# Gate stages with bias rows per item and one-hot row choice, and another end of the first mixture

## The reference

```python
x = x + L0_gnn(layernorm(x), edges)      # three message rounds, then attention over nodes
x = x + L0_ffn(layernorm(x))             # 8 experts, hidden 1536, two per node
x = x + L1_gnn(layernorm(x), edges)      # two graph attention layers, 8 heads and 1
x = x + L1_ffn(layernorm(x))             # 4 experts, hidden 384, one per node

# L0_ffn
gates = softmax(x @ Wg + bg)
topg, topi = top_k(gates, 2); topg = topg / sum(topg)
h = gelu(x @ W1[e] + b1[e]);  y = h @ W2[e] + b2[e]
out = sum over the two chosen experts of topg * y
# L1_ffn: the same with argmax of the logits and a share of 1
```

## Time and profile before

| | us |
|---|---|
| median of 3 runs | 1471.71 |
| lowest and highest run | 1467.08, 1474.52 |
| the profiled execution | 1465.52 |
| its span, first to last instruction | 1463.0 |

### The profile page before, as it was taken

How to read it: one execution, slowest core, us unless ns; L and a number is a source line. 1 busy time by engine, 2 the same in 40 slices (tenths; PEclk the granted TensorE clock), 3 DMA queues, 4 the chain that set the end, 5 groups by cost and what they waited for, 6 DMA issues and landing times.

```text
span 1463.0 us, 18209 instructions
## 1 busy us (share of the span) xinstructions
PE 1287.5 (88%) x6567; PEld 1088.3 (74%) x6567; DVE 920.1 (63%) x1748; ACT 560.8 (38%) x981; POOL 127.4 (9%) x114
## 2 busy tenths in 40 slices
PE   5999999999999899986788999999966687967786
PEld 3677489799699766566588999999955587946543
DVE  4477655554644655546459999999965798244213
ACT  2111313413512333450058888888831364010010
POOL 0000200000000000110200000000060563010101
PEclk9999999999999999997599999999987889976699
DMA  9320462203105200313258999999961000010276
GB/s 334 133 86 29 173 216 108 98 1 141 65 1 216 87 1 1 113 40 130 86 216 295 370 379 377 385 371 373 355 225 51 25 1 1 0 65 1 97 253 209
DMA packets 81778, 223.46 MB, mean 153 GB/s; under 512 B 4972, under 2 KB 18348, under 8 KB 81592
## 3 DMA queue, kind: packets, MB, share of 16 engines
q1 hardware_dynamic: 75256, 192.79, 36.1%
q0 software_dynamic: 6464, 29.89, 5.6%
HBM read 195.92 MB, written 26.74 MB: 152 GB/s over the span
## 4 chain that ended last, share of the span: by engine, by line
PE 71%; DVE 16%; DMA 5%; issue 3%; ACT 2%; POOL 2%; ACTq 0%; SPq 0%; DVEq 0%; POOLq 0%
PE dve_ps L720 10%; PE dve_ps L721 10%; PE dve_ps L722 10%; PE dve_ps L763 4%; PE act_ps L720 3%; PE act_ps L721 3%; PE act_ps L722 3%; PE dve_ps L809 3%; DMA slot<-in_e1w 2%; PE act_ps L936 2%; PE dve_ps L953 2%; PE act_ps L760 2%; DVE part_slot L2041 2%; PE dve_ps L1175 2%; DVE part_slot L2032 2%
## 5 line engine op out<-in xcount | busy, mean ns | idle before, releaser
L2032 DVE TENSOR_TENSOR part_slot<-slot,item_hi 128x768 fp32r<-128x768 f32 x156 | 137.7, 951 | 0.9 <-ACT item_hi L1499 0.8
L1499 ACT ACTIVATE item_hi<-slot 128x768 fp32r<-128x768 f32 x156 | 118.0, 838 | 34.2 <-DMA slot<-in_e0w 31.5
L2041 DVE TENSOR_TENSOR part_slot<-slot,item_hi 128x768 fp32r<-128x768 f32 x132 | 116.5, 952 | 0.0
L720 PE MATMUL act_ps<-item_hi,hid_hi 128*128 128x384 f32 x288 | 98.8, 343 | 4.8 <-DVE hid_lo L2209 4.8
L1507 ACT ACTIVATE item_hi<-slot 128x768 fp32r<-128x768 f32 x132 | 100.0, 877 | 7.0 <-DMA slot<-in_e0w 6.8
L720 PE MATMUL dve_ps<-item_hi,x_hi 128*128 128x384 f32 x288 | 98.3, 341 | 2.9 <-DVE part_slot L2032 1.7
L721 PE MATMUL act_ps<-part_slot,hid_hi 128*128 128x384 f32 x288 | 99.0, 344 | 0.0
L722 PE MATMUL act_ps<-item_hi,hid_lo 128*128 128x384 f32 x288 | 97.7, 339 | 0.0
L721 PE MATMUL dve_ps<-part_slot,x_hi 128*128 128x384 f32 x288 | 97.2, 337 | 0.0
L722 PE MATMUL dve_ps<-item_hi,x_lo 128*128 128x384 f32 x288 | 96.9, 337 | 0.0
L1390 ACT ACTIVATE h_t<-act_ps,par 128x256 f32<-128x256 f32 x36 | 21.1, 587 | 122.4 <-PE act_ps L827 122.4
(11 more groups left out here) (395 smaller groups left out, 3254.6 us busy)
## 6 DMA issues: line engine op xcount, KB each, us to landing
slot<-in_e0w SPq DMA_DIRECT2D x48, 2304.0 KB, 10.3
slot<-in_w SPq DMA_DIRECT2D x9, 2304.0 KB, 9.6
slot<-in_e1w SPq DMA_DIRECT2D x12, 1152.0 KB, 6.2
ea_raw<-in_edge SPq DMA_DIRECT2D x8, 1024.0 KB, 5.4
slot<-in_wqkv SPq DMA_DIRECT2D x3, 2304.0 KB, 15.2
item_x<-xs SPq DMA_DIRECT2D x17, 384.0 KB, 9.7
xs<-zrow POOLq DMA_DIRECT2D x2, 3072.0 KB, 15.7
ys<-item_y POOLq DMA_DIRECT2D x16, 384.0 KB, 6.3
```

The source lines that it names most:

```text
L720: mm(to, kept[0], moved[0], start=start, stop=False)
L1499: go(item_hi[j][k][:, :], slot[s][:, k * D:(k + 1) * D], ACT.Copy).then_inc(up_high[j], 1)
L2032: vv.tensor_tensor(part_slot[s][:, ks], slot[s][:, ks], item_hi[j][k][:, :].bitcast(F32), ALU.subtract).then_inc(up_low[j], 1)
L2041: vv.tensor_tensor(part_slot[s][:, ks], slot[s][:, ks], item_hi[j][k][:, :].bitcast(F32), ALU.subtract).then_inc(down_low[j], 1)
```

## The change

**Bias rows.** The stages bias0 and bias1 go: no gates are turned, no biases multiplied or added to x. Instead POOL loads the second bias of an item's expert, one row of 768, to all 128 partitions (`b2row`) after it has issued the store of the item before, and VectorE adds it as it copies the result (waiting for `b2_in`).

**Gate stages by tile.** Tiles are turned one by one (`turn_tile`), copied by ScalarE in two halves, and each tile's logits made apart (`tile_logits`). Stage 0 norms tiles 0 and 1 together, then 2, then 3; stage 1 each alone, with the last weighted sums between the turns. The low parts of the first item's up weights move: slot 2's on VectorE ahead of the additions, slot 3's to POOL. Counts are made in 5 products (`rank_tokens`).

**Row choice.** ScalarE and VectorE keep high and low parts of the normed rows, not turned. `first_sel[0]` is made straight from the counts (the rank within expert 0, and chosen by expert 0) before the rest of the plan; `first_sel[1]` holds item 1's rows. `pick_rows` chooses rows of item 0 and of item 1 with 16 single-pass products of 384 columns each; ScalarE copies them to `item_x`, and TensorE turns them. Item 1 is no longer loaded from DRAM, and the scatters are waited for only before item 2 (in the second mixture before the loop). TensorE's order is: choose 0, turn 0, first up half, choose 1, second up half, turn 1.

**Loop.** Hidden blocks go in the order 0, 1, 2 and not 2, 0, 1; gelu and high part alternate; the second up half waits for all three bent blocks of the item before; the result is taken after three of the six last low parts.

**End of the first mixture, and the products h1 and h2.** VectorE and not POOL makes the low parts of the next weight, six before the first gathered addition and six after it; then the last result, a gathered addition, and the distributed rows tile by tile with statistics; one `rescale` of all four tiles follows. The first unit of h1 and of h2 waits block by block.

```diff
-            def gates(run, xt, ne, stage, bias_stage, b2, k_in):
...
+            def turn_tile(run, t, source, before):
+                pe.wait_ge(normed, before + t + 1)
+                if t >= 2:
+                    pe.wait_ge(kept_act, 7 * run.layer + 2 * (t - 1))
+                for half in range(2):
+                    bank = act_ps[(2 * t + half) % RING]
+                    for j in range(3):
...
+                    turned.then_inc(tile_turned, 1)
...
+            def rank_tokens(run):
+                pe.wait_ge(run.sel_set, 1)
+                ne = run.ne
+                mm(run.count_bank[:, 0:(NT + 1) * ne], tri[:, :], sel[:, :, 0:ne], start=True, stop=False)
+                for t in range(1, NT + 1):
+                    last = mm(run.count_bank[:, t * ne:(NT + 1) * ne], ones[:, :], sel[:, 0:NT + 1 - t, 0:ne], start=False, stop=(t == NT))
+                last.then_inc(counts_ready, 1)
+            def pick_rows(run, i, highs, lows):
...
+                pe.wait_ge(first_set[i], run.layer + 1)
+                for half in range(2):
+                    hs = slice(half * HALF, (half + 1) * HALF)
+                    for m in range(NT):
+                        for part in (highs, lows):
+                            picked = mm(run.pick_banks[half][:, 0:HALF], first_sel[i][:, m, :], part[m][:, hs],
+                                        start=(m == 0 and part is highs), stop=(m == NT - 1 and part is lows))
+                    picked.then_inc(picked_rows, 1)
+            for t in range(3):
+                turn_tile(run0, t, xn1, NT * (L + 1))
...
+            tile_logits(run0, 0, xn1_t)
+            turn_tile(run0, 3, xn1, NT * (L + 1))
+            for t in range(1, NT):
+                tile_logits(run0, t, xn1_t)
...
-                            pe.wait_ge(hid_bent, 3 * (i - 1) + 1)
+                            pe.wait_ge(hid_bent, 3 * i)
...
-                pick_x()
-                times_up(0)
+                pick_rows(run, 0, xn1_hi, xn1_lo)
+                turn_x(0)
+                times_up(0, (0,))
+                pick_rows(run, 1, xn1_hi, xn1_lo)
+                times_up(0, (1,))
                 turn_x(1)
```

```diff
-            normalise(xres, xn1, attention_arrives)
+            low_up(0, 0)
+            for ts in ((0, 1), (2,), (3,)):
+                for t in ts:
+                    for half in range(2):
+                        add_to_x("wo", t, half)
+                    gate_rows(t, xres)
+                rescale(ts, xres, xn1)
+            keep_turned(run0, xn1_t)
+            for t in range(NT):
+                low_rows(run0, t, xn1, xn1_hi, xn1_lo)
...
+                for t in range(NT):
+                    last = vv.tensor_scalar(first_sel[0][:, t, :], slot_iota[:, :], count[:, t, 0:1], sel[:, t, 0:1], ALU.is_equal, ALU.mult)
...
                 def result(i):
                     wait(dve, run.y_out, 16 * i)
+                    dve.wait_ge(run.b2_in, 16 * (i + 1))
                     dve.wait_ge(down_used[1], DC * (i + 1))
                     for half in range(2):
-                        vv.tensor_copy(item_y[:, half * HALF:(half + 1) * HALF], down_banks[half][:, 0:HALF]).then_inc(y_set, 1)
+                        hs = slice(half * HALF, (half + 1) * HALF)
+                        vv.tensor_tensor(item_y[:, hs], down_banks[half][:, 0:HALF], b2row[:, hs], ALU.add).then_inc(y_set, 1)
...
-                    low_up(1, k + 2)
+                    low_up(1, k + 2, range(3))
                     result(k)
+                    low_up(1, k + 2, range(3, DC))
...
+            for i in range(DC):
+                low_first(i)
+            add_gathered(0)
+            for i in range(DC, 2 * DC):
+                low_first(i)
+            last_result()
+            add_gathered(1)
+            result_rows(0)
+            result_rows(1)
+            for t in range(2, NT):
                 add_gathered(t)
-            vv.memset(root[:, 0, :], 0.0).then_inc(parts_added, 1)
-            last_result()
-            normalise(xres, xn2, results_arrive)
+                result_rows(t)
+            rescale(range(NT), xres, xn2)
...
+            def load_b2(run, e):
+                pool.dma_start(b2row[:, :], run.b2[bass.ds(e, 1), :].rearrange("a d -> (a d)").partition_broadcast(P)).then_inc(run.b2_in, 16)
...
+            for k in range(DC):
+                ks = slice(k * D, (k + 1) * D)
+                pool.wait_ge(up_high[1], k + 1)
+                nc.gpsimd.tensor_tensor(part_slot[3][:, ks], slot[3][:, ks], item_hi[1][k][:, :].bitcast(F32), ALU.subtract
+                                        ).then_inc(up_low[1], 1)
...
                 with pool.Fori(1, last) as k:
                     store(k, *stored_at(k))
+                    load_b2(run, expert(k + 1))
```

466 lines of the change are left out of this document (255 added, 211 removed).

## The result

The changed kernel takes 1399.12 us (median of four runs, 1396.34 to 1404.01) where the kernel before took 1469.39 on the same chip: a ratio of 0.9525, 95% interval 0.9501 to 0.9549, faster by 70 us. The forecast (1414, range 1394 to 1441, faster) held, but the time lies 15 us under its centre and 2 over rival (a): the sum of terms was 10.6 us short.

The account below looks back on a forecast made before the run. Gate stages were bound by chained waits between engines, the loop by full TensorE and DMA engines. Terms 30.2 + 8.4 + 4 + 23.7 - 8.5 - 3 = 54.8 us gave 1410.7 or 1416.5 by base; forecast 1414, range 1394 to 1441.

Parts of the forecast that it names:

- rival (a): Bias rows are free and the clock stays up in the gate stages: 11.5 + 6 us more gain, about 1397; 14%.
- Gate stage 0: Before the first loop: logits 7.7 us earlier, counts 4.1, counts to loop 18.4; 30.2 us gained in all.
- The loop: First mixture's items: bias row's 0.39 MB an item at 375 GB/s costs +8.5 us; +3.4 if 385 were the ceiling.
- The end of the first mixture: Last result to h1: first product of h1 8.4 us earlier, 0.7 of it from the first low hidden block coming sooner.
- h2: Product h2 starts 0.8 us after its first low block instead of behind eight: 4 us gained.
- Gate stage 1: Before the second loop: logits about 4.7 us earlier, counts 4.0, counts to first up product 15.0; 23.7 us gained.
- Second loop: Second mixture: five bias rows at 1.0 us each join the loop, half to all showing; +3 us cost.
- (b): In the loop, waiting for three bent blocks couples ScalarE's lateness in: +24 us, about 1438; 17%.
- (c): The loop's bias row lands late, so VectorE's result and TensorE's next down half wait; slower than before, 1480 at 30 us; 5%.
- (d): The loop ends when its loads do, so the early start is given back wholly: 30.2 us back, 1444; 3%.

Follow-up runs that it names:

- low_dve: The changed kernel with slot 3's six low parts made on VectorE instead of POOL; ratio 0.9504 to the kernel before.
- plain4: The changed kernel with three further 0.39 MB loads an item of the first mixture, each reading 128 different rows of expert weights; ratio 0.9735, items 29.47 us apart.
- before_row: The kernel before with one unused bias row loaded for each item of the first mixture on POOL's queue; ratio 1.004, items 27.72 us apart.
- order201: The changed kernel with hidden blocks in the old order 2, 0, 1 and the second up half waiting for one bent block; ratio 0.9517.
- warm: The changed kernel with 14, 14 and 6 unused 384-column products in three idle stretches of TensorE in gate stage 0; ratio 0.948.
- best: The changed kernel with unused TensorE products in both gate stages, slot 3's low parts on VectorE and the first mixture's end norm in two parts; 1391.99 us, ratio 0.9485.

## Why the prediction held, and where it was short

**Gate stage 0** (30.2 predicted, 29.6 measured) is right step by step, to 0.6 us in each: two stretched operations (run low_dve took them away and got 2.25 us back for the 2 that were charged), logits at the lower clock, five products for fourteen, then the dependence of the first item on nothing but the counts. The hidden turn was put 28.8 us behind the counts and came 28.6 behind. That the choice of item 1 pays was in the sum as 2.9 us of TensorE against the load from DRAM; alone it is worth 2.65. The load's 8.78 us of the earlier trace rows were not what there was to win: it runs beside the second up half, and TensorE stood idle for it 3.13 us in the kernel before.

**The loop** is the step that failed. The prediction's "At 375 GB/s, the middle of the loop's slices ..., 10.61 MB take 28.3 us" took a rate that TensorE's pace had asked for (10.22 MB in 27.20 us) as what the queues can give. Plain loads got 401 GB/s over 180 us. The page "DMA: Bandwidth & Descriptors" of the Trainium skill (section Measured), which has about 425 GB/s, was set aside in the prediction for the trace's rate. No run here held that figure in the loop (401 GB/s over 180 us is the most, in plain4), but its answer, that the row is free, was nearer than the one taken. Measured, the row costs 0.5 us an item in the kernel before (5 us in ten items, 5.9 in the ratio) and nothing that can be seen in the changed one. The changed loop loses 1.2 us between item 0's hidden turn and item 11 for 8.5 predicted, and the run without rows shows the same pace. Measured by low hidden parts, items are 27.25 to 27.5 apart in all changed kernels with at most one row. That is neither the row nor the order of blocks, and it is about 1 us in all: at the turns of rows the changed kernel has 27.26 and low_dve, which loads the rows too, (1021.22 - 776.84) / 9 = 27.15, as the kernel before. What makes this 1 us is open. Other differences of the loop (gelu and high part in turn, the result taken between two halves of low parts) were not tried alone, and of the kernel before there is one trace. Why this loop hides a row that the one before does not is open for the same reason. Two sums of the prediction were also off: at 385 GB/s its own terms give 10.61 / 0.385 = 27.56 us an item and 10 x 0.50 - 2.7 = +2.3 us, not +3.4, and the median less 54.8 is 1416.9, not 1416.5; neither moves the forecast.

**The end of the first mixture** (8.4 predicted, 7.6 measured): the last result came 1.0 us behind the start of the last down product and not 0.5, because the gathered addition waited 3.5 us for its rows and pushed the six low parts behind it into the result's way. That the one norm costs is borne out with 0.7 us. The old order of hidden blocks makes no difference at h1, so the 0.7 us that the sum gave for it is not shown there. **h2**: 3.4 measured, 4 predicted.

**Gate stage 1** (27.5 measured, 23.7 predicted): logits 6.1 us earlier for 4.7, counts 3.8 for 4.0, from counts to the first up product 17.6 for 15.0. What made the logits 1.4 us better was not traced. The last is a term of the clock: the sum had all of the choice and the first up products at the lower level, and the clock rose within the choice, so that the 12 records of up products took 4.11 us.

**Second loop** (-3 predicted, -1.5 measured): right in sign, and too small to be held against single traces, as the stretch from the first up product to the last hidden copy took 57.9 to 64.4 us in profiles in which this code is the same, or all but the same. It was put down to rows joining the weights on the queues; the part that shows in the changed kernel's trace is all behind the last hidden copy (26.75 us for 23.7). Run before_row, whose second mixture is that of the kernel before, has 26.0 there, so these 3 us are not shown to come from the change at all.

**Rivals.** (a) got the time: the row was nearly free and the clock rose earlier in stage 1, though it stayed low in stage 0. (b) is out by order201. (c) did not occur: in both loops rows landed in 3.7 to 7.9 us, and in the first no result waited. The prediction read the page "SBUF — State Buffer" of the Trainium skill (section SBUF: two separate sides) too widely: the page says that the descriptors cannot be written while VectorE runs an operation in a two-port mode, such as an fp32 copy within SBUF, and not whenever VectorE is busy. In this loop VectorE, busy 175 of 180 us, subtracts (two inputs) or reads PSUM, and this trace shows no such wait for these loads. (d) occurred in small: of 6.5 us of further early start in warm, about 1 went at item 1's weights.

## What to carry to other kernels

A DMA rate read beside a busy TensorE can be a demand and not a ceiling, even where the DMA share reads 1.00, as here; put further loads in, and see at which rate the pace breaks. Where a stage is a chain of small steps between engines, look for what the first consumer needs and cut the rest out of its way: here that gave 18.6 and 17.6 us, where nine products saved in the counts gave 3.9. A wait that is the longest in a view can still be free: ask what ends last behind it.

## What the runs showed of the hardware that was not expected

- One row of DRAM sent to 128 partitions is dearer than 128 rows of the same size: three such loads an item cost 30.90 us of pace, three plain ones 29.47, so 0.48 us more for each 0.39 MB.
- Unused products in TensorE's idle stretches pay for themselves. With 14 large products in a 3.27 us idle stretch the 36 records of small ones after it took 5.21 and 4.08 us in two profiles, for 7.69 without; with an idle stretch of 1.98 us left open in stage 1 the 24 records after it ran at the lower level again, and 8 products put in at that level took 2.91 us and held up the counts.
- TensorE's clock fell without a gap of the engine ahead of it: in warm to 1.2 GHz between 683 and 684 us, within 36 records of small products and with TensorE busy since 674.2; it went back to 2.4 behind large ones. In the 48 small records of the earlier trace rows it fell with TensorE busy since 684.54. In best it stayed up through the same 36 records and fell 0.8 us behind them; why not within them these runs do not tell.
